# A graph kernel on one core: the source rows of 16 of 392 edge tiles fetched row by row from the SP queue

## The reference

```python
messages = features[src] * edge_weight[:, None]
aggregated = jax.ops.segment_sum(messages, dst, num_segments=N_NODES)
out = act(features * aggregated @ W1 + b1) + act(aggregated @ W2 + b2)
...
x = _layernorm(x + out * rsqrt(sum(out * out)))
# second layer: two GELU products on the neighbours' rows, weighted segment sum, two GELU products, layernorm
```

## Time and profile before

| | us |
|---|---|
| median of 3 runs | 3035.27 (3031.89 to 3040.17) |
| the profiled execution's own time | 3019.24 |
| its span | 3017.4 |
| first stage within the span | 0 to 1278.3 |
| second stage | 1278.3 to about 2600 |
| last stage | from about 2600 |

### The profile page before, as it was taken

The page is one execution under the profiler, slowest core; times in us unless marked ns, Lnnn a source line. Parts: engine busy times, 40 slices in busy tenths (PEclk is TensorE's granted clock), DMA queues, the critical chain, the costliest instruction groups (busy, mean ns, idle before and its releaser), DMA issues. The chain is left out here.

```text
span 3017.4 us, 39223 instructions
## 1 busy us (share of the span) xinstructions
PE 2161.6 (72%) x11956; PEld 1702.2 (56%) x11956; DVE 2204.7 (73%) x5529; ACT 1066.6 (35%) x1964; POOL 2383.8 (79%) x1774
## 2 busy tenths in 40 slices
PE   3046555555554553279898989989989998699997
PEld 3035555455454553257676666667667766466664
DVE  5079988888888886368777777777777777288888
ACT  0000000000000000045444444445445454288887
POOL 7678888888888888658888888888888887488888
PEclk8555555555555555589999999999999999699998
DMA  9898888888887766467776777776777676356664
GB/s 229 203 208 191 171 174 180 180 182 175 170 183 166 157 147 138 71 179 180 172 176 162 170 175 167 164 175 164 172 171 175 159 175 136 83 192 207 208 206 157
DMA packets 1036086, 516.47 MB, mean 171 GB/s; under 512 B 540544, under 2 KB 998336, under 8 KB 1035880
## 3 DMA queue, kind: packets, MB, share of 16 engines
q1 hardware_dynamic: 764616, 372.57, 47.1%
q0 software_dynamic: 144256, 77.17, 18.4%
q10 hardware_dynamic: 127008, 64.23, 7.5%
HBM read 269.97 MB, written 243.84 MB: 170 GB/s over the span
## 5 line engine op out<-in xcount | busy, mean ns | idle before, releaser
L300 PE MATMUL sums<-xg,weigh 128*128 128x64 f32 x1960 | 435.0, 418 | 518.0 <-ACT ms L323 380.9
L544 POOL DMA_INDIRECT state<-ms,sidx x392 | 657.2, 1677 | 157.4 <-issue 114.3
L256 POOL DMA_INDIRECT table<-ms,sidx x392 | 622.5, 1588 | 140.9 <-issue 115.2
L300 PEld LDWEIGHTS sums<-xg,weigh 128*128 128x128 f32 x1960 | 420.5, 327 | 551.7 <-issue 485.1
L368 DVE TENSOR_SCALAR weigh<-rowp,key,ew 128x128 f32<-128x128 f32 (+3 forms) x784 | 424.0, 603 | 167.7 <-PE rowp L288 160.1
L530 POOL DMA_INDIRECT box<-table,node_dst x392 | 397.7, 1015 | 128.6 <-issue 112.8
L243 POOL DMA_INDIRECT xg<-in_x,node_src x392 | 383.1, 977 | 120.8 <-issue 104.6
L323 ACT ACTIVATE ms<-sums 128x256 f32<-128x256 f32 x98 | 37.6, 384 | 1143.1 <-DMA table<-ms,sidx 1057.6
L374 DVE SCALAR_TENSOR_TENSOR seen<-rowp,key,earlier 128x128 f32<-128x128 f32 (+3 forms) x784 | 383.3, 544 | 0.0
L735 DVE SCALAR_TENSOR_TENSOR leaky<-z_p,bz,leaky 128x512 f32<-128x512 f32 x294 | 219.7, 748 | 212.4 <-ACT leaky L656 210.1
L577 PE MATMUL z_p<-turned_s,wz 128*128 128x512 f32 x588 | 325.9, 638 | 2.8 <-DVE leaky L735 1.6
(11 more groups left out here) (93 smaller groups left out, 3553.4 us busy)
## 6 DMA issues: line engine op xcount, KB each, us to landing
box<-table SPq DMA_DIRECT2D x97, 768.0 KB, 5.0
joins<-weigh ACTq DMA_DIRECT2D x98, 640.0 KB, 3.8
weigh_in<-joins SPq DMA_DIRECT2D x98, 640.0 KB, 6.8
table<-rows SPq DMA_DIRECT2D x97, 512.0 KB, 5.3
pair<-state SPq DMA_DIRECT2D x97, 512.0 KB, 3.9
xin<-in_x SPq DMA_DIRECT2D x97, 256.0 KB, 6.1
state<-y SPq DMA_DIRECT2D x97, 256.0 KB
out<-y SPq DMA_DIRECT2D x97, 256.0 KB, 2.2
```

What stands on the lines that cost most here:

```text
L256: pool.indirect_dma_start(out=table[:, :], out_offset=bass.IndirectOffsetOnAxis(ap=sidx[0][:, i:i + 1], axis=0), in_=ms[k % MR][:, b, :], ...
L300: last = pe.matmul(sums[k % 2][:, a * D:(a + 1) * D], block_of(0, k, b)[:, a * P:(a + 1) * P], xg[:, k * WT + b, :], start=b == a, stop=b ...
L544: pool.indirect_dma_start(out=state[:, :], out_offset=bass.IndirectOffsetOnAxis(ap=sidx[1][:, at:at + 1], axis=0), in_=ms[k % SM][:, b, :] ...
```

## The change

Four windows (32, 54, 76 and 95: `PICKED`), 16 tiles, are taken out of POOL's gathers. Their 2,048 rows are fetched by SP. For each of the 512 pairs of a picked window and a partition, `pick(n)` loads the partition's four node numbers from `node_src` into registers of SP by one load with bounds 0 and N-1, and then issues four transfers, each of one 256 B row of x at an address made from a register, into one partition of `xg`. The picks are spread evenly over rounds 0 to 89 (`NCH - 8`), 5 or 6 a round, behind `load_x` and ahead of `clear`. PE waits for a picked window's rows on a semaphore of that window. POOL's other gathers keep their order, spread anew over the same rounds.

```diff
--- before.py
+++ after.py
@@ -51,6 +51,8 @@
     TP = TAIL // TG
     STEPS = max(NWIN, NCH)
     EARLY = 28 * WT
+    PICKED = (NWIN // 3, NWIN * 5 // 9, NWIN * 7 // 9, NWIN - 3)
+    LISTED = [w for w in range(NWIN) if w not in PICKED]
     BEFORE_SCATTER = 3
 
 
@@ -161,10 +163,11 @@
                     if k < COARSE:
                         return k // 4, 16 * WT * 4
                     pair = (k - COARSE) // 2
-                    of = min(2, NWIN - COARSE - 2 * pair)
+                    of = min(2, len(LISTED) - COARSE - 2 * pair)
                     return COARSE // 4 + pair % RING, 16 * WT * (2 * (pair // RING) + of)
 
                 gathered = [sem(f"gathered0_{q}") for q in range(COARSE // 4 + RING)]
+                picked = [sem(f"picked{w}") for w in range(len(PICKED))]
                 summed, taken, scattered = sem("summed0"), sem("taken0"), sem("scattered0")
 
 
@@ -200,6 +203,15 @@
                             sp.wait_ge(copied, c + 1)
                             sp.dma_start(to.rearrange("(g p) f -> p g f", g=g),
                                          rows2[c % TR][0:p, 0:g, :, :].rearrange("p g a f -> p g (a f)")).then_inc(built[c % TR], 16)
+
+                        def pick(n):
+
+                            w, p = n // P, n % P
+                            t = PICKED[w] * WT
+                            _, rows = nc.values_load_multi_w_load_instructions(
+                                node[0][p:p + 1, t:t + WT], engines=(mybir.EngineType.SP,), min_val=0, max_val=N - 1)
+                            for b in range(WT):
+                                sp.dma_start(xg[p:p + 1, t + b, :], x[bass.ds(rows[b], 1), :]).then_inc(picked[w], 16)
 
                         def clear(rows, at, p, g, done):
                             sp.dma_start(rows[at:at + p * g, :].rearrange("(p g) f -> p g f", g=g), zeros[0:p, 0:g, :]).then_inc(done, 16)
@@ -228,6 +240,8 @@
                             store_rows(c0)
                             if c0 + XR < NCH:
                                 load_x(c0 + XR)
+                            for n in range(len(PICKED) * P * c0 // (NCH - 8), min(len(PICKED) * P * (c0 + 1) // (NCH - 8), len(PICKED) * P)):
+                                pick(n)
                             if c0 % 3 == 2 and c0 // 3 < len(later):
                                 clear(state_rows[:, 1, :], *later[c0 // 3], zeroed)
                         for piece in later[(NCH - 3) // 3 + 1:]:
@@ -239,13 +253,14 @@
 
                     @block.gpsimd
                     def _(pool):
-                        def gather(i):
+                        def gather(j):
+                            i = LISTED[j // WT] * WT + j % WT
                             pool.indirect_dma_start(out=xg[:, i, :], out_offset=None, in_=x[:, :],
                                                     in_offset=bass.IndirectOffsetOnAxis(ap=node[0][:, i:i + 1], axis=0),
-                                                    ).then_inc(gathered[arrival(i // WT)[0]], 16)
+                                                    ).then_inc(gathered[arrival(j // WT)[0]], 16)
 
                         def upto(k):
-                            return min(EARLY + (TILES - EARLY) * k // (NWIN - 4), TILES)
+                            return min(EARLY + (len(LISTED) * WT - EARLY) * k // (NWIN - 4), len(LISTED) * WT)
 
                         def scatter(k):
                             pool.wait_ge(taken, k + 1)
@@ -292,8 +307,11 @@
                         def join(k):
 
                             pe.wait_ge(weighed, turn[0, k] + 1)
-                            q, landed = arrival(k)
-                            pe.wait_ge(gathered[q], landed)
+                            if k in PICKED:
+                                pe.wait_ge(picked[PICKED.index(k)], 16 * WT * P)
+                            else:
+                                q, landed = arrival(LISTED.index(k))
+                                pe.wait_ge(gathered[q], landed)
                             wait(pe, taken, k - 1)
                             for a in range(WT):
                                 for b in range(a, WT):
```

## The result

| | before | changed |
|---|---|---|
| median | 3034.86 us (4 runs) | 4020.98 us (4 runs, 4011.3 to 4026.8) |
| ratio | | 1.325, 95% interval 1.3225 to 1.3278 |
| span of the profiled execution | 3017.4 | 4017.1 |
| end of the first stage in it | 1278.3 | 2271.7 |

The change makes the kernel 986 us slower. In the two traces the first stage is 993.3 us longer and the rest 6 us. The sign and the mechanism were forecast; the stage's growth was forecast as 577 us.

A forecast was written before the change was run, and what follows sets the result against it. POOL was taken to bound the first stage, with SP taking over: 161.85 + 270 + 1331.2 = 1763, plus 92 gives 1855, +577 us. From 3019.24 that gives 3596, plus 16 is 3612; forecast 3610, range 3050 to 4200.

The forecast's parts named there:

- POOL bounds the first stage; 16 gathers are worth 20.7 us: First stage: POOL is busy or issuing throughout; each gather costs it 1.293 us, so 16 gathers removed are worth 20.7 us.
- the best case: Rival: SP fits its picks in and POOL gives back 20.7 us, giving 3015 us; chance 9 in 100.
- SP sets the stage if its round is longer than POOL's: SP's list in the first stage: rounds of 17.8 us in place of 11.0, stage +577 us; chance 76 in 100.
- the other signs: Expected in the changed profile's first stage: POOL's busy share about 55%, DVE waiting for `xin`, SP's rounds about 18 us.
- The transfers themselves cost nothing: DMA engines: the same 2,048 rows of 256 B still move, so their work was costed at nothing either way.
- One row, 0.40 us; one load, 1.0: SP's list: a pick is one register load at 1.0 us plus four rows at 0.40 each, 2.6 us.
- my dearest rival: SP's picks cost over 3.7 us each, from separate loads or checks or delayed issues; over 4200 us, chance 8 in 100.
- The rest of the round 3.0 us, the tail 92.3 us: SP's store, load and clears take 3.0 us a round; 92.3 us pass from SP's last picking round to stage end.
- Break-even at 1.43 us a pick: First stage: SP keeps up with POOL, ending the stage at 1257.6 us, only if a pick costs at most 1.43 us.
- the forecast's sum: First stage: 161.85 + 90 x 3.0 + 512 x 2.6 = 1763 us, plus 92, ends at 1855 instead of 1278.
- The two rules of the Trainium skill: A 0.6 us `tensor_load` floor would give about 3407; usually small sequencer savings would make SP fit, 9 in 100.

The follow-up runs named there:

- 512 fixed rows: Against the kernel before: window 95 fetched from SP's queue by 512 transfers of fixed rows, without register loads or address arithmetic; 3026.8 against 3017.8 us (1.0023).
- fixed rows: Against the changed kernel: all 2,048 row transfers read fixed rows of x, without register load, check or address arithmetic; 3102.1 us (1.022 of the kernel before).

## Why the prediction came out as it did

- *POOL bounds the first stage; 16 gathers are worth 20.7 us.* The bound was right. The worth was 11 us, in part since the gathers cover the landing of scatters. It did not matter to the forecast, only to the best case, if nothing else got dearer: "faster" could have been 0.36% at most.
- *SP sets the stage if its round is longer than POOL's.* Shown by SP's vanished waits, and by the runs that took its instructions away: without the checks 485 us came back, without loads, checks and addresses 919. Of the other signs, POOL's busy share fell to 43% of the stage, not 55, since the stage got longer than forecast, and DVE waits for `xin`.
- *The transfers themselves cost nothing.* Nearly right for the DMA engines; 512 fixed rows cost 0.23% with SP mostly waiting.
- *One row, 0.40 us; one load, 1.0.* This is the step that was mis-sized. Issue and address together were (591 + 310) / 2048 = 0.44, near the 0.40. The load was 0.72. But the bounds check, for which I had counted a 0.04 us gap inside the row's 0.40, is a compare of 0.15 us and an assert of 0.02 with gaps, 0.265 a number, 1.06 a pick, 543 us. A pick came to 3.54 us in place of 2.6: +483 us. The trace of before has no compare on a sequencer, and I gave it the price of the only gap that I could see. With 3.54, the pick came near the 3.7 at which my dearest rival began, to which I gave 8 in 100.
- *The rest of the round 3.0 us, the tail 92.3 us.* 2.5 and 56.4 (2215.3 to 2271.7), -45 and -36 us. Behind its last pick SP issues loads and stores at once, and ACT's copies then follow each other at 9.7 us. With the late start, +14, the terms give 577 + 483 - 45 - 36 + 14 = 993, as measured; the terms are parts of that one measured stage, so this is no second proof.
- *Break-even at 1.43 us a pick.* No run had 512 picks at that price. The nearest, fixed rows at 1.59 us (814 over 512), lost 66 us where the forecast's sum gives 59, so for SP's list it was about right. It was too generous as a rule for gain, since 128 picks with SP far from full still lost 0.5%.
- *The two rules of the Trainium skill.* It gives a floor of about 0.6 us for a `tensor_load` ("DMA: Bandwidth & Descriptors", "Latency and other measured facts"). The median of 0.561 in the changed kernel is near it, but as a floor it does not hold here: without row transfers in front the median was 0.308. By the Trainium skill ("DMA: Bandwidth & Descriptors", "Issuing engines are not separate DMA queues"), issuing from several engines saves only a usually small time on the sequencer. Here that time was not small: issue and address took 1.76 us a pick, with load and checks 3.54, and this set the stage.

## What to carry to other kernels

A transfer that another engine's queue takes over costs that engine's list of instructions, all of them: count what the call expands to. With their gaps, compares, asserts and address steps took 0.07 to 0.2 us each, an issue 0.29 and a load 0.72. The 21 instructions for four rows of 256 B came to 3.5 us, while one gather of 128 such rows costs POOL 1.3 us. An engine that waits for three quarters of a stage has spare time only between its deadlines; here it also carried the x loads on which every other engine depends, and clears whose place in the round seems to matter. Before moving work off the bound engine, take it away altogether in one run: what that gives is the ceiling, and here it was 11 us.

## What the runs showed of the hardware

- A runtime check of a loaded number costs SP 0.27 us with its gaps, nearly as much as the issue of a 256 B transfer at 0.29.
- A register load from SBUF took 0.31 us at the median with no row transfers about, 0.56 between them, and 1.2 straight behind a bulk load of x in the changed kernel.
- With fixed rows, the first row's issue straight behind a load of x took 1.5 us at the median and 3.8 at most. A 512 KB store issued straight behind a 1 MB clear took 4.1 us at the median in the changed kernel and 6.3 with fixed rows; the kernel before has a wait between the two.
- SP's instructions took 0.70 us each with as much between from about 150 to 180 us, in the traces from two chips and in that of the changed kernel, and not in those from two other chips and in the first trace of the kernel before; 14 us in all. No cause was found.
